# First expert's rows of the last batch summed into PSUM, and scatters moved to one unit of a group

## The chip, the cores and the metric

The kernel runs on one core of a Trainium2 chip. The metric is the device time of one execution in microseconds (us). The five engines are PE (TensorE: matmuls and weight loads), DVE (VectorE), ACT (ScalarE), POOL (GpSimd) and SP (SyncE, which here only issues DMAs). TensorE runs at one of two clock levels, 1.2 or 2.4 GHz; the profile's PEclk is the granted share of 2.4 GHz.

## The reference, cut to what matters

```
x = x + attention(layernorm(x))      # x: 4 batches x 512 tokens x 256, 32 query heads, 8 KV heads
y = layernorm(x)                     # mixture of experts, 8 experts, top 2
gates = softmax(y @ gating_w); topk_w, topk_idx = top_k(gates, 2)
position = running count of the items of an expert, in token order; valid = position < 640
buf[expert, position] = y[token]     # 8 experts x 640 slots x 256
h = relu(buf @ w1 + b1); out_e = h @ w2 + b2
out = x + sum over the token's two experts of weight * out_e[expert, position]
```

An expert has CAP = 640 slots. A slot holds a token's normalised row (256 numbers), its token number and the gate weights of the 8 experts (ROW = 265 numbers). The slots of the first expert, number 0, are rows 0 to 639 of the DRAM tensor slot_rows.

## The kernel before

**Attention.** The work goes in 32 groups (4 batches x 8 KV heads, g = 0 to 31) of 16 units each; a unit is 128 query rows of one head. The function all_periods (line 331) writes the order out by hand: in unit n of group g every engine runs its step for n of this group, for n - 16 of the next group, for n + 16 of the group before and for n + 32 of the one before that. So projections of the next group (PE, lines 1298 to 1329), the rotations of its query and key chunks (POOL, lines 614 to 630), and the product of probabilities and values of the group before (PE, line 1383, in units 4, 6 and 8) lie among the scores of this group (PE line 1365, DVE lines 1021 and 1030, ACT line 765). Rotation Q23 lies in unit 2, KV and Q01 of the next group in units 4 and 5. POOL's residual addition (line 659) of an earlier group lies in unit 6, the sink term (line 642) in unit 15, the denominator (line 652) in unit 0 after it. On ACT the sink's exponential (line 785) stands in unit 15.

**Routing.** While batch b + 1 is in attention, the steps route(r, b) with r = 0 to 121 run beside it, r = 16 * (g % 8) + unit: transposes (line 1452), statistics, gate logits (line 1464), top 2, the count of items per expert (PE lines 1475 to 1481), the slot numbers (DVE lines 1172 to 1196), the gate weights (line 1197) and the normalised rows (ACT line 895). Then POOL scatters the rows into slot_rows with eight indirect DMAs of 128 rows (line 676). SCATTER_AT places them, two at a time: r = 99 and 115 are unit 3 of the seventh and eighth group, r = 105 and 121 their unit 9. For the last batch nothing is left to run beside, so line 347 runs r = 0 to 121 one after the other with last = True.

**Experts.** After the last scatter has landed, SP loads the 640 rows of expert 0 (line 541), then those of expert 1, and the weights of expert 1 (lines 550, 553). PE runs two matmuls that only keep its clock up (line 1493), transposes the rows into banks 0 to 2 (turn_slots, line 1502), ACT and DVE split them into a high and a low part (slots_hi line 940, slots_lo line 1249), and PE makes the hidden layer (to_hidden, line 1524), transposes the rows of the next expert, and makes the output rows (to_rows, line 1537). DVE adds b2 (line 1268), ACT multiplies by the gate weight (line 958) and POOL adds the rows to the output with indirect DMAs (line 709). The slots of expert e + 1 are loaded once the rows of expert e - 1 have been added (line 540). On DVE, hidden_split (lines 1258, 1260) stands beside to_hidden.

## Time and profile before

| | us |
|---|---|
| median of 3 runs (1098.31 to 1101.82) | 1098.95 |
| the profiled execution's own time | 1099.66 |
| its span, first to last instruction | 1097.9 |
| PE busy, share of the span | 1041.9, 95% |
| DVE busy | 869.7, 79% |
| POOL busy | 706.1, 64% |
| ACT busy | 654.5, 60% |

The spans are counted from the first instruction. Attention ends at about 813 us, the routing of the last batch lies between about 817 and 837 us, and the experts fill the rest. A busy share is a mean over these three parts, so it says little of any of them; what matters is which wait ends last in each.

### The profile page before, as it was taken

How to read it: one execution, taken by the hardware profiler on the slowest of the kernel's cores; microseconds unless marked ns; L12 is line 12 of the kernel's file. 1: busy time of each engine (PE TensorE's matmuls, PEld its weight loads, DVE VectorE, ACT ScalarE, POOL GpSimd, SP SyncE). 2: the span in 40 equal slices, each digit the busy share in tenths (PEclk: the TensorE clock that was granted, in tenths of full speed). 3: DMA queues.
4: the chain of work that ended last, by engine and by line, in shares of the span. 5: the costliest groups of instructions: out<-in, count | busy, mean ns of one | idle time of the engine just before them, and what ended most of it. 6: DMA issues, size and time to landing. Idle time of an engine off the chain costs nothing.

```text
span 1097.9 us, 32754 instructions
## 1 busy us (share of the span) xinstructions
PE 1041.9 (95%) x13282; PEld 747.8 (68%) x13282; DVE 869.7 (79%) x1929; ACT 654.5 (60%) x1662; POOL 706.1 (64%) x586
## 2 busy tenths in 40 slices
PE   7999999999999999999999999999883999999995
PEld 4466666666666666666666666666562999999995
DVE  7999999999899999999998999898861455555441
ACT  4666667666677666676766666676631555545441
POOL 5658766767666787666788676667732454555662
PEclk9999999999999999999999999999996999999998
DMA  4555554433333333432334333232524044444321
GB/s 111 155 132 127 132 145 123 125 90 96 93 84 95 102 98 80 118 79 77 85 104 119 85 99 97 68 91 73 161 77 156 18 118 122 121 122 112 90 59 21
DMA packets 115399, 111.46 MB, mean 102 GB/s; under 512 B 35216, under 2 KB 103888, under 8 KB 115120
## 3 DMA queue, kind: packets, MB, share of 16 engines
q1 hardware_dynamic: 97504, 89.61, 29.8%
q0 software_dynamic: 7296, 8.55, 4.7%
q10 hardware_dynamic: 10448, 11.20, 3.5%
q8 instruction: 105, 1.72, 0.7%
q14 instruction: 46, 0.38, 0.1%
HBM read 74.17 MB, written 21.83 MB: 87 GB/s over the span
## 4 chain that ended last, share of the span: by engine, by line
PE 53%; DVE 37%; issue 4%; DMA 2%; ACT 1%; POOL 1%; SPq 0%; POOLq 0%; DVEq 0%
PE bank L1383 20%; DVE probs_ring L1021 16%; DVE probs_t L1030 14%; PE bank L1365 10%; PE bank L1537 9%; PE bank L1524 9%; DVE heads_sb L1050 4%; PE bank L1502 1%; PE bank L1415 1%; PE bank L1307 1%; DMA slots<-slot_rows 1%; PE bank L1324 1%; PE bank L1342 1%; POOL out L709 1%; PE bank L1464 1%
## 5 line engine op out<-in xcount | busy, mean ns | idle before, releaser
L765 ACT ACTIVATE probs_ring<-probs_ring,neg_max 128x512 f32<-128x512 f32 x512 | 365.8, 717 | 227.0 <-DVE neg_max L1021 220.1
L1021 DVE CUSTOM_DVE_ANT_0 probs_ring<-bank,mask,sink_neg 128x512 f32<-128x512 f32 x512 | 360.0, 736 | 31.9 <-PE bank L1365 30.3
L1030 DVE STREAM_TRANSPOSE probs_t<-probs_ring 128x1024 f32<-128x1024 f32 x256 | 317.2, 1239 | 0.2 <-ACT probs_ring L765 0.2
L1365 PE MATMUL bank<-qk_st 64*128 64x512 f32 x1024 | 281.2, 625 | 12.7 <-DVE neg_max L1021 8.1
L1383 PE MATMUL bank<-probs_t,v_quads 32*64 32x256 f32 x8192 | 254.5, 381 | 1.5 <-DVE probs_t L1030 0.7
L1383 PEld LDWEIGHTS bank<-probs_t,v_quads 32*64 32x64 f32 x8192 | 181.9, 132 | 81.9 <-issue 54.5
L624 POOL TENSOR_TENSOR chunk_sb<-chunk_sb,rope_sb 128x512 f32<-128x512 f32 (+1 forms) x94 | 119.8, 1274 | 128.3 <-issue 100.4
L1365 PEld LDWEIGHTS bank<-qk_st 64*128 64x128 f32 x1024 | 85.2, 186 | 78.3 <-DVE neg_max L1021 43.1
L629 POOL TENSOR_TENSOR qk_st<-chunk_sb,swap_sb 128x512 f32<-128x512 f32 (+1 forms) x94 | 120.2, 1279 | 7.4
L1415 PEld LDWEIGHTS bank<-wo_sb,heads_sb 64*128 64x128 f32 x992 | 96.1, 187 | 37.5 <-issue 29.2
L625 POOL TENSOR_TENSOR swap_sb<-swap_sb,rope_sb 128x512 f32<-128x512 f32 (+1 forms) x94 | 120.0, 1276 | 0.0
L1415 PE MATMUL bank<-wo_sb,heads_sb 64*128 64x256 f32 x992 | 117.4, 376 | 0.0
L1537 PE MATMUL bank<-w_part,hidden_hi 128*128 128x256 f32 x640 | 115.6, 284 | 0.0
L1324 PE MATMUL bank<-xcur,w_hi 64*128 64x512 f32 x496 | 100.6, 479 | 0.0
L682 POOL TENSOR_TENSOR w_lo<-w_raw,w_hi 128x2048 fp32r<-128x2048 f32 x8 | 36.9, 4609 | 96.6 <-ACT w_hi L844 96.6
L1537 PEld LDWEIGHTS bank<-w_part,hidden_hi 128*128 128x128 f32 x640 | 98.7, 189 | 0.1
L765 ACT ACTIVATION_READ_ACCUMULATOR probs_ring<-probs_ring,neg_max 128x1 f32 x512 | 97.2, 190 | 0.0
L950 ACT ACTIVATE hidden<-bank,b_sb 128x320 f32<-128x320 f32 x128 | 60.5, 524 | 54.1 <-PE bank L1524 54.1
L1537 PE MATMUL bank<-w_part,hidden_lo 128*128 128x256 f32 x320 | 90.5, 283 | 0.0
L1268 DVE TENSOR_TENSOR expert_sb<-bank,b_sb 128x256 f32<-128x256 f32 x40 | 17.0, 424 | 82.7 <-PE bank L1537 75.4
L659 POOL TENSOR_TENSOR x_sb<-x_sb,y_sb 128x512 f32<-128x512 f32 x62 | 79.2, 1277 | 4.5
L709 POOL DMA_INDIRECT out<-expert_sb,slots x40 | 64.1, 1602 | 26.9 <-ACT expert_sb L958 17.2
(162 smaller groups left out, 1474.5 us busy)
## 6 DMA issues: line engine op xcount, KB each, us to landing
v_quads<-v_rows SPq DMA_DIRECT2D x128, 128.0 KB
recip_wide<-recip_rows SPq DMA_DIRECT2D x64, 256.0 KB
w_raw<-in_L_ffn_w SPq DMA_DIRECT2D x14, 1024.0 KB, 8.4
swap_sb<-chunk_sb SPq DMA_DIRECT2D x314, 32.0 KB
w_raw<-in_L_attn_W_qkv SPq DMA_DIRECT2D x32, 256.0 KB, 2.9
slot_rows<-x2T ACTq DMA_DIRECT2D x8, 662.5 KB, 5.8
slots<-slot_rows SPq DMA_DIRECT2D x8, 662.5 KB, 4.0
w_raw<-in_L_attn_W_qkv SPq DMA_DIRECT2D x64, 64.0 KB, 2.8
```

Of the source, the lines that this page charges most:

```text
L624: nc.gpsimd.tensor_tensor(straight, straight, rope_sb[rows, 0, :], ALU.mult).then_inc(s_pool, 1)
L625: nc.gpsimd.tensor_tensor(swapped, swapped, rope_sb[rows, 1, :], ALU.mult).then_inc(s_pool, 1)
L629: nc.gpsimd.tensor_tensor(qk_st[j][rows, PAIRS if c == KV else c - Q01, :], straight, swapped, ALU.add).then_inc(s_rot, 1)
L765: nc.scalar.activation(probs[(g * UNITS + n) % RING][:, :], probs[(g * UNITS + n) % RING][:, :], ACT.Exp, bias=neg_max[j][:, n:n + 1], sca ...
L1021: nc.vector.tensor_tensor_reduce(probs[(g * UNITS + n) % RING][:, :], SCORE[SCORE_OF[n // 2][n % 2]][:, :], mask[:, L - P - t * P:2 * L - ...
L1030: nc.vector.transpose(probs_t[j][:, :, (h // 2) * (2 * P):(h // 2 + 1) * (2 * P)] .rearrange("p b (h q) -> p h b q", h=2)[:, :, :, t * BLK ...
L1324: ins = nc.tensor.matmul(chunk_bank(c)[:, :], w[rows, kc, chunk_cols(c)], xcur[g // NKV % 2][rows, part, kc, :], start=(second == 0 and kc ...
L1365: nc.tensor.matmul(SCORE[SCORE_OF[n // 2][hh]][:, :], qk_st[j][half, h // 2, t * P:(t + 1) * P], qk_st[j][half, PAIRS, :], start=True, sto ...
L1383: ins = nc.tensor.matmul(PV[a][p * HD:(p + 1) * HD, 0:2 * P], v_quads[j][rows, d, c * HD:(c + 1) * HD], probs_t[j][rows, blk, p * 2 * P:(p ...
L1415: ins = nc.tensor.matmul(PV[a][:, 0:D], heads_sb[rows, a, h * P:(h + 1) * P], wo_sb[rows, (g % NKV) * 2 + h, :], start=(half == 0 and h == ...
L1524: ins = nc.tensor.matmul(banks[4 + 2 * (c % 2) + half][:, 0:HALF], w[:, kc, c * P:(c + 1) * P], a[:, at:at + HALF], start=(kc == 0 and m = ...
L1537: ins = nc.tensor.matmul(FFN2[s][:, 0:D], a[:, c, s * P:(s + 1) * P], w[:, c, :], start=(c == 0 and m == 0), stop=(c == HC - 1 and m == 2))
```

## The change

In words. (1) After the scatters of the first three batches have landed, SP loads the rows of expert 0 that are in slot_rows by then (slots[0], "old rows"). In the last batch's routing PE fills banks 0 to 2 with zeros by a product with a zero column and adds the transposes of the old rows, written as ordinary fp32 products with the identity. (2) DVE makes a 0/1 matrix for each of the four tiles of the last batch (select, 128 tokens x 640 slots: 1 where the token's slot in expert 0 equals the slot number, which POOL writes with an iota). ACT makes the high part of the normalised rows (last_hi) and DVE the low part (last_lo). PE multiplies both by select and adds them into the same banks: 8 times 4 matmuls. So banks 0 to 2 hold what turn_slots(0) gave before, and to_hidden(0) no longer waits for the scatters, the load or the transposes of expert 0. (3) The rows of expert 1 are loaded first once the last scatter has landed, and expert 0's full rows (for token numbers and gate weights) behind them. (4) The weights of expert 1 are loaded before the scatters are waited for. b1 is loaded and transposed earlier, b1 and b2 have semaphores of their own. (5) The two keep_warm matmuls ahead of turn_slots(0) are gone. (6) SCATTER_AT puts two scatters in r = 89 and three each in r = 105 and 121, all of them unit 9 of a group (the sixth, seventh and eighth). (7) In SBUF slots and qk_st[0] are placed elsewhere.

```diff
-        SCATTER_AT = {99: (0, 1), 105: (2, 3), 115: (4, 5), 121: (6, 7)}
+        SELECT_AT = 72
+        SCATTER_AT = {89: (0, 1), 105: (2, 3, 4), 121: (5, 6, 7)}
...
             recip_out(GROUPS - 2)
             recip_spread(GROUPS - 2)
+            sp.wait_ge(s_rot, GROUPS * CHUNKS)
+            sp.dma_start(b1_rows[:, :], b1.rearrange("e (c p) -> (e c) p", p=P)).then_inc(s_b1_in, 16)
+            sp.wait_ge(s_scores, (GROUPS - 1) * UNITS)
+            sp.wait_ge(s_scattered, (B - 1) * (16 * TPB * TOPK))
+            sp.dma_start(slots[0][:, :, :], slot_rows_of(0)).then_inc(s_old_in, 16)
             recip_out(GROUPS - 1)
             recip_spread(GROUPS - 1)
             out_init(B - 1)
...
+            weights_in(1)
 
             sp.wait_ge(s_scattered, 16 * TILES * TOPK)
+            slots_in(1)
+            sp.wait_ge(s_slots_turned, 3)
             slots_in(0)
-            sp.wait_ge(s_slots_in[0], 16)
-            for e in range(E - 1):
-                slots_in(e + 1)
...
+            for e in range(2, E):
+                slots_in(e)
+                weights_in(e)
...
             def pool_route(r, b, last):
+                if r == TURN_X_LAST and last:
+                    pool.wait_ge(s_residual, 2 * GROUPS)
+                    nc.gpsimd.iota(slot_numbers[:, :].rearrange("p (s q) -> p s q", s=SLOTT), pattern=[[1, SLOTT], [SLOTT, P]],
...
                 if r == WEIGHTS_AT and last:
-                    norm2(b, 0)
+                    for t in range(TPB):
+                        norm2(b, t)
+                        nc.scalar.activation(last_hi[:, t, :], x_sb[:, b * TPB + t, :], ACT.Identity,
+                                             bias=norm_bias[:, t:t + 1], scale=rstd[:, t:t + 1]).then_inc(s_last_hi, 1)
                     act.wait_ge(s_neg_top, b + 1)
                     nc.scalar.activation(gates[:, :, :], gates[:, :, :], ACT.Exp).then_inc(s_gate_exp, 1)
-                    for t in range(1, TPB):
-                        norm2(b, t)
...
             def weigh(e):
+                if e == 0:
+                    act.wait_ge(s_slots_in[0], 16)
...
+                if r == SELECT_AT and last:
+                    dve.wait_ge(s_place, b + 1)
+                    step(nc.vector.scalar_tensor_tensor(place_key[:, :], prefix[:, :, 0], 1.0,
+                                                        chosen[:, :, 0].bitcast(F32), ALU.add, ALU.mult))
+                    dve.wait_ge(s_slot_numbers, 1)
+                    for t in range(TPB + 1):
+                        if t < TPB:
+                            nc.vector.tensor_scalar(select[:, t, :], slot_numbers[:, :], place_key[:, t:t + 1], None,
+                                                    ALU.is_equal).then_inc(s_select, 1)
+                        if t > 0:
+                            dve.wait_ge(s_norm2, b * TPB + t)
+                            dve.wait_ge(s_last_hi, t)
+                            nc.vector.tensor_tensor(last_lo[:, t - 1, :], xn2[:, t - 1, 0:D],
+                                                    last_hi[:, t - 1, :].bitcast(F32), ALU.subtract).then_inc(s_last_lo, 1)
...
+            def old_rows(bank):
+                nc.tensor.matmul(banks[bank][:, :], ones_r[:, :], before_r[:, 0:1].broadcast_to([P, 512]),
+                                 start=True, stop=False)
+                for m in range(bank * 4, min(bank * 4 + 4, KC * SLOTT)):
+                    kc, s = divmod(m, SLOTT)
+                    nc.tensor.matmul(slot_cols(kc, s, s + 1), slots[0][:, s, kc * P:(kc + 1) * P], identity[:, :],
+                                     start=False, stop=False)
+
+            SLOT_PIECES = [(0, 0, 4), (0, 4, 5), (1, 0, 3), (1, 3, 5)]
+
+            def last_rows(t, part):
+                rows = (last_hi, last_lo)[part]
+                for i, (kc, s0, s1) in enumerate(SLOT_PIECES):
+                    final = t == TPB - 1 and part == 1
+                    ins = nc.tensor.matmul(slot_cols(kc, s0, s1), rows[:, t, kc * P:(kc + 1) * P],
+                                           select[:, t, s0 * P:s1 * P], start=False, stop=final and i != 1)
...
             def pe_route(r, b, last):
+                if r == LOGITS_AT + 1 and last:
+                    pe.wait_ge(s_old_in, 16)
+                    pe.wait_ge(s_residual, 2 * GROUPS)
+                    old_rows(0)
+                    old_rows(1)
+                if r == SELECT_AT and last:
+                    pe.wait_ge(s_centred, B)
+                    old_rows(2)
+                    for i in range(2 * TPB):
+                        t, part = ((0, 0), (1, 0), (0, 1), (2, 0), (1, 1), (3, 0), (2, 1), (3, 1))[i]
...
-            pe.wait_ge(s_bias_in, 32)
-            pe.wait_ge(s_place, B)
-            nc.tensor.transpose(PV[3][:, 0:E * HC], b1_rows[:, :], identity[0:E * HC, 0:E * HC]).then_inc(s_b1_turned, 1)
-
-            pe.wait_ge(s_scattered, 16 * TILES * TOPK)
-            keep_warm(2, PROJ, x_sb[:, 0:2, :])
-
...
-            turn_slots(0)
             pe.wait_ge(s_b1, 1)
```

## Rows read from the trace of the kernel before

**Rows 1.** The page, chain that ended last, shares by engine.
```profile
PE 53%; DVE 37%; issue 4%; DMA 2%; ACT 1%; POOL 1%; SPq 0%; POOLq 0%; DVEq 0%
```

**Rows 2.** Chain of waits from last routing to first output rows: start, us, what.
```profile
824.25 0.19 DVE prefix L1175
...
826.41 0.20 DVE xn L370
...
839.13 3.97 DMA slots<-slot_rows
...
846.83 14.33 PE bank L1524 x96
...
861.30 1.28 PE bank L1502 x10
862.58 14.24 PE bank L1537 x120
```

**Rows 3.** Timeline of POOL: a scatter in group 31; first and last of the last batch.
```profile
785.70 1.00 POOL L676 DMA_INDIRECT slot_rows<-xn,scatter_idx  x1
...
827.55 1.00 POOL L676 DMA_INDIRECT slot_rows<-xn,scatter_idx  x1 [20.21 <-DVE xn L370]
...
836.57 0.98 POOL L676 DMA_INDIRECT slot_rows<-xn,scatter_idx  x1 [0.30 <-issue]
```

**Rows 4.** Timeline of PE: last output projection, and logits of the last routing.
```profile
813.53 3.72 PE L1404 MATMUL bank<-wo_sb,heads_sb 128*128 128x256 f32 x16 [0.92 <-DVE heads_sb L1050]
...
818.59 1.91 PE L1464 MATMUL bank<-gate_sb,x2T 128*128 128x8 f32 x16
```

**Rows 5.** Busy time by window; the eighth value (PEclk) is TensorE's granted clock.
```profile
821.00:822.00 1.00, 0.00 (x0) 0.00 (x0) 0.93 (x11) 0.98 (x2) 0.00 (x0) 0.50 0.77 270
...
844.00:845.00 1.00, 1.00 (x8) 1.00 (x6) 0.01 (x1) 0.60 (x1) 0.00 (x0) 0.58 0.89 164
```

**Rows 6.** Lines 1258 and 1260 on DVE: duration in ns, min/median/max.
```profile
L1258 DVE CAST hidden_hi<-hidden x64: 493/494/682, 849.8 to 1072.6; 128x640 fp32r<-128x640 f32 x64
...
L1260 DVE TENSOR_TENSOR hidden_lo<-hidden,hidden_hi x64: 824/826/849, 850.4 to 1073.1; 128x640 fp32r<-128x640 f32 x64
```

**Rows 7.** Timeline of ACT: normalised rows of the last batch.
```profile
823.85 0.60 ACT L895 ACTIVATE xn<-x_sb,norm_bias,rstd 128x256 f32<-128x256 f32 x1 [1.32 <-DVE norm_bias L1160]
...
824.51 1.57 ACT L895 ACTIVATE xn<-x_sb,norm_bias,rstd 128x256 f32<-128x256 f32 x3
```

**Rows 8.** Line 709 on POOL, the scatter-adds beside the experts, ns min/median/max.
```profile
L709 POOL DMA_INDIRECT out<-expert_sb,slots x40: 1544/1554/1907, 874.7 to 1087.8; - x40
```

**Rows 9.** Timeline of POOL, the sink term once in a group: start of groups' ends.
```profile
358.31 0.21 POOL L642 TENSOR_TENSOR sink_arg<-neg_max,sink_all 128x16 f32<-128x16 f32 x1 [2.94 <-DVE neg_max L1021]
...
407.98 0.21 POOL L642 TENSOR_TENSOR sink_arg<-neg_max,sink_all 128x16 f32<-128x16 f32 x1 [0.91 <-DVE neg_max L1021]
...
431.87 0.21 POOL L642 TENSOR_TENSOR sink_arg<-neg_max,sink_all 128x16 f32<-128x16 f32 x1 [2.12 <-DVE neg_max L1021]
...
554.62 0.21 POOL L642 TENSOR_TENSOR sink_arg<-neg_max,sink_all 128x16 f32<-128x16 f32 x1 [1.61 <-DVE neg_max L1021]
...
604.39 0.21 POOL L642 TENSOR_TENSOR sink_arg<-neg_max,sink_all 128x16 f32<-128x16 f32 x1 [0.82 <-DVE neg_max L1021]
...
752.46 0.22 POOL L642 TENSOR_TENSOR sink_arg<-neg_max,sink_all 128x16 f32<-128x16 f32 x1 [1.63 <-DVE neg_max L1021]
...
803.05 0.21 POOL L642 TENSOR_TENSOR sink_arg<-neg_max,sink_all 128x16 f32<-128x16 f32 x1 [0.84 <-DVE neg_max L1021]
```

**Rows 10.** Timeline of PE: probability-value products, without and with scatters just before.
```profile
417.50 2.41 PE L1383 MATMUL bank<-probs_t,v_quads 32*64 32x256 f32 x80
...
786.82 3.51 PE L1383 MATMUL bank<-probs_t,v_quads 32*64 32x256 f32 x80
```

**Rows 11.** Timeline of ACT behind the sink term of group 16, without scatters.
```profile
432.85 0.20 ACT L785 ACTIVATE sink_exp<-sink_arg 128x16 f32<-128x16 f32 x1
...
436.56 0.60 ACT L747 ACTIVATE chunk_sb<-bank 128x512 f32<-128x512 f32 x1 [1.30 <-PE bank L1324]
```

More of the change, by code:

```diff
@@ L246, in moe_layer @@
         v_next = sb("v_next", [P, TPB, HD], c=actx)
-        qk_st = [sb(f"qk_st{i}", [P, PAIRS + 1, L], c=actx) for i in range(2)]
+        qk_st.append(sb("qk_st1", [P, PAIRS + 1, L], c=actx))
         v_quads = [sb(f"v_quads{i}", [P, TPB, TPB * HD], c=actx) for i in range(2)]
@@ L274, in moe_layer @@
         b1_sb = sb("b1_sb", [P, E, HC], c=mctx)
+        sb("behind_rope", [P, 320], c=mctx)
+        slots = [sb(f"slots{i}", [P, SLOTT, ROW], c=mctx) for i in range(2)]
         b2_sb = sb("b2_sb", [P, E, D], c=mctx)
@@ L277, in moe_layer @@
         w2_hi, w2_lo = w2_parts[0::2], w2_parts[1::2]
-        slots = [sb(f"slots{i}", [P, SLOTT, ROW], c=mctx) for i in range(2)]
         slots_hi = sb("slots_hi", [P, KC * CAP], F32R, c=mctx)
@@ L281, in moe_layer @@
         hidden = [sb(f"hidden{i}", [P, CAP], c=mctx) for i in range(2)]
+        lctx = ExitStack()
+        slot_numbers = sb("slot_numbers", [P, CAP], c=lctx)
+        place_key = sb("place_key", [P, TPB], c=lctx)
+        select = sb("select", [P, TPB, CAP], F32R, c=lctx)
+        last_hi = sb("last_hi", [P, TPB, D], F32R, c=lctx)
+        last_lo = sb("last_lo", [P, TPB, D], F32R, c=lctx)
+        lctx.close()
         hidden_hi = sb("hidden_hi", [P, HC, CAP], F32R, c=mctx)
@@ L1265, in rows_out @@
                     dve.wait_ge(s_added, e * SLOTT * 16)
+                else:
+                    dve.wait_ge(s_b2_in, 16)
                 for s in range(SLOTT):
@@ L1437, in _, with slot_cols @@
             turn_v(0)
-            def pe_route(r, b, last):
+            def slot_cols(kc, s0, s1):
+                m = kc * SLOTT + s0
+                return banks[m // 4][:, m % 4 * P:(m % 4 + s1 - s0) * P]
+            def old_rows(bank):
[12 more added lines that the diff above has]
+                                           select[:, t, s0 * P:s1 * P], start=False, stop=final and i != 1)
+                    if final and i != 1:
+                        ins.then_inc(s_slots_turned, 1)
+            def pe_route(r, b, last):
+                if r == LOGITS_AT + 1 and last:
[8 more added lines that the diff above has]
+                        t, part = ((0, 0), (1, 0), (0, 1), (2, 0), (1, 1), (3, 0), (2, 1), (3, 1))[i]
+                        if part == 0:
+                            pe.wait_ge(s_select, t + 1)
+                            pe.wait_ge(s_last_hi, t + 1)
+                        else:
+                            pe.wait_ge(s_last_lo, t + 1)
+                        last_rows(t, part)
                 if r in TURN_X_AT:
```

51 lines of the change are left out of this document (33 added, 18 removed).

## The prediction

> **What bounds the kernel now.** I read the page first: its chain of waits lies on PE and DVE for 90% of the span and on DMA, POOL and issuing for a few per cent [rows 1]. These few per cent are what the change is about, so I went to the chain in order of time. Behind the last attention group it runs over DVE's routing to the slot numbers (824.25) and the gate weights, which end at 826.61, then over eight scatters on POOL, their landing, the load of expert 0's rows (839.13 to 843.10), their transposes, and reaches the first hidden matmul at 846.83; the output rows of expert 0 start at 862.58 [rows 2]. The eight scatters are issued 1.288 us apart, from 827.55 to 836.57 [rows 3], and the load starts at 839.13, so from gate weights to landed scatters it is 12.5 us, and 4.0 more for the load. PE does nothing useful in it.
>
> The second place is in attention. A group takes 23.89 us from one sink term to the next where nothing is scattered (407.98 to 431.87, group 16). Groups 14 and 15 take 49.67 together, 22 and 23 take 49.77, 30 and 31 take 50.59 [rows 9]. Twice 23.89 is 47.78, so the three pairs of groups in which scatters stand cost 1.89, 1.99 and 2.81 us extra, 6.69 in all. Where it is lost is seen on PE: a block of 80 probability-value matmuls takes 2.41 us in group 16 and 3.51 in group 31 [rows 10], where the first scatter of unit 3 had been issued at 785.70, 1.1 us before the block [rows 3]. PE waits for no semaphore inside such a block; the rows show when the stall comes, not what makes it. That is 1.1 us a hit, and a hit in each of the six groups gives 6.6 of the 6.69.
>
> **Part one, the last batch.** I count on the clock of the profiled execution, with attention unshifted.
>
> Old rows on PE begin at 820.50, when the logits end [rows 4]. The nearest row is line 1404: eight fp32 matmuls (16 records) of 256 columns in 3.72 us [rows 4], 0.465 each. A 128-column one is taken as half, 0.23; eight are 1.9 us. Two fills of 512 columns cost 0.24 each, from 14.24 us for 120 matmuls of 256 columns [rows 2]. Sum 2.3 us, to 822.8, just when the count can start anyhow. But the granted clock fell to 0.50, the 1.2 GHz level, by 821 [rows 5], after PE had done nothing but transposes and 8-column matmuls since 817. At that level the old rows take up to 4.7 us and count and slot numbers come up to 1.9 us later. At the lower end, nothing. I take 0.7, nearer to the low end because the new matmuls fill the very stretch in which PE stood still before.
>
> Then DVE, on which all the new work stands ahead of picks, indices and gate weights. Slot numbers end at 824.44 [rows 2], plus 0.7 is 825.15. place_key is a small instruction, 0.2. Four select instructions go by the 128x640 cast, 0.52 with issue; upper bound is the 128x640 two-operand form, 0.83 [rows 6], which would add 1.2 us. Four last_lo of 128x256 go by the same two-operand row, 0.83 cut from 640 to 256 columns by the sum of a fixed part and a column part: about 0.38. Sum 3.6, to 828.95. ACT must not be later: norm rows and last_hi are eight activations at 0.52, from 823.85 [rows 7], so the last last_hi is ready at 828.05; the exponential of the gates behind them ends at 828.3, before DVE asks for it. POOL's iota waits for the last residual at 818 and has six us of cover; its price if late is its own length, about 1 us. So DVE ends last_lo at 828.95 instead of beginning the picks at 824.47: all that followed there, 2.14 us to the gate weights, now ends at 831.1, 4.5 us later than 826.61.
>
> PE meanwhile: eight last_rows of 1280 columns, at 0.119 per 256 columns 0.6 each; the last two need the last lo part, so PE ends at about 830.2. ACT's three hi parts follow; DVE's three lo parts come behind the gate weights, 831.1 plus 1.7 (1280 columns, twice the 128x640 form [rows 6]), so the hidden layer can begin at 832.8 instead of 846.83. It takes 14.33 [rows 2], to 847.1.
>
> The scatters are still there and start 4.5 us later: the load that started at 839.13 starts at 843.6, and its rows, now expert 1's, are in at 847.6. **Both paths meet within half a us**, and the later one counts: transposes of expert 1 (1.28 [rows 2]) from 847.6, output rows of expert 0 at 848.9 instead of 862.58. That is **13.7 us** gained. It is not the 14 us of the transfer that vanish: the transfer is there, but it lies beside expert 0's hidden layer. What comes behind has the same order and the same spacing as before, so the 235 us from there on stay. Expert 0's full rows are loaded right behind expert 1's and are wanted first when its rows are weighed, over 14 us later.
>
> Costed at nothing: the weights of expert 1, 2 MB. By the load of 662 KB in 3.97 us [rows 2] they need about 12.6 us; issued near 820 they are in at 833, beside the first scatters, and are first read after expert 0's hidden layer at 847. If they held up the scatters, each us is a us of the end. b1's transpose lies in front of the last probability-value block, where PE waits for DVE. The load of the old rows stands on SP ahead of the last reciprocals' DMA; it waits for the third batch's scatters, issued by 792, and the reciprocals are due at 805. If those scatters landed after 805, the heads would be late by the difference. The two keep-warm matmuls lay beside the load, so nothing is gained by leaving them out; what they did, the new matmuls must do. Before, the clock was granted at 0.50 until it came back between 844 and 845 [rows 5], ahead of the first hidden matmul.
>
> **Part two, the scatters.** Those of unit 3 go; nothing replaces them there. Unit 9 now has two in groups 13, 21, 29 and three in the six groups from 14 on. A scatter costs POOL 1.29 [rows 3], three are 3.9 us. In group 16 POOL stood idle for 2.12 us before its sink term [rows 9], so it is 1.8 late with three. ACT reads the sink term 0.77 after its end (432.08 to 432.85), and 3.7 us later ACT waits 1.30 us for PE [rows 11]: of 1.8 late, 0.77 is slack and the remaining 1.0 falls into those 1.30. So I charge nothing; the bound above is 1.0 in five groups, 5.0 us. In group 31 POOL has no rotations left and reaches unit 9 early, when PE is still in its last block; I leave one hit there, 1.1. So part two gives 6.69 - 1.1 = **5.6 us**; the lower bound is 0.6, with the lateness above charged in full.
>
> **Sum.** 13.7 + 5.6 = 19.3 us. On the profiled execution's own 1099.66 (span 1097.9 and 1.8 around it) that is 1080.4; the median of the runs stands 0.7 lower, so 1079.7.
>
> **Two rules weighed.** The stalls of rows 10 stand in a block of many short instructions. The Trainium skill (Runtime: NRT & Kernel Launch, Instruction fetch mechanics) says of instruction fetch that it is hidden because the sequencer dispatches more slowly than its buffer fills. By that rule moving a DMA could not speed PE by way of the fetch; the rows show a us lost there whatever its name, and by the rule alone part two would give nothing.
>
> The new scatters run beside DVE's hidden split, the old ones beside an idle DVE. The nearest row is line 709: 40 indirect DMAs in the expert part, median 1554 ns, longest 1907 [rows 8]; at the longest, eight scatters lose 8 x 0.35 = 2.8 us, my upper bound. The Trainium skill (SBUF — State Buffer, The "DVE blocks DMA" trap, with its figures under A bandwidth-pool intuition that's wrong) says that such a DMA cannot get its descriptors written while DVE runs a copy of the two-port kind, and gives about 3.1 us instead of 0.62. An estimate by that page is 8 x 3.1 in place of 8 x 1.29, 14.5 us more, with 1094 as the end. Rows 8 speak against it.
>
> **Rivals.** (a) Part one as told, part two gives nothing or the third scatter's lateness comes through: 1079.7 + 5.0 to 5.6, about **1085**. For it: POOL's idle time is smaller than three scatters. Against: two scatters of unit 9 already left only 0.9 idle and cost no more [rows 9]. (b) The clock stays at 1.2 GHz through the last rows: 8 x 0.6 becomes 8 x 1.2 and starts near 827, hidden layer at about 838.5, its first us also slow, a loss of 6 to 7: **1086**. For it: the clock fell at just this place [rows 5]. Against: PE is now busy almost without a break. (c) **Slower.** POOL's scatters are held by DVE's hidden split beside them, in the 14 us of expert 0's hidden layer. Expert 1's rows then come late and PE waits ahead of turn_slots(1). It decides from 19.3 / 8 = 2.4 us more per scatter; at 4.0 us each, 8 x 2.7 = 21.7 lost: **1101**. (d) It does not do what it says: the old rows or the b1 wait hold PE past the scatters' landing, so that part one gives nothing: 1099.66 - 5.6 - 0.7 = **1093**; the loads would have to be 10 us late.
>
> **Chances.** Forecast 0.73, (a) 0.14, (b) 0.07, (c) 0.03, (d) 0.03. The range 1076.0 to 1086.0 takes in (a) and (b); below, it has part one without the 0.7, both paths at their best (0.6), part two in full (1.1) and a stall or two less in the expert part. About 0.3% (3.3 us) can be told from no change. Faster 0.96, same 0.01, slower 0.03.
>
> **What would show it.** First hidden matmul near 833 minus part two's shift of 5.6, so 827; the output rows of expert 0 near 843; transposes of expert 1 waiting for their load by less than 1 us; scatters of the last batch 1.3 us apart. Blocks of 80 in groups 14, 15, 22, 23 back at 2.4 to 2.7 us, groups at 23.9. Wrong would be: sink terms that ACT waits for, the granted clock at 0.50 beyond 826, scatters over 1.6 us apart, or a long wait for expert 1's slots.

## The result: 1086.97 us, 1.2% faster, and 7 us short of the forecast

| | kernel before | changed kernel |
|---|---|---|
| median of the runs on the same chip | 1100.24 us (1098.31 to 1101.82, 4 runs) | 1086.97 us (1085.54 to 1088.03, 4 runs) |
| span of the profiled execution | 1097.9 us | 1086.2 us |
| mean granted TensorE clock | 0.981 | 0.988 |

Ratio 0.9879, 95% interval 0.9856 to 0.9903. The direction was right; the time lies 0.97 us above the range.

The span is 11.7 us shorter. It can be cut in three, at the start of the last heads_sb products (the end of attention) and at expert 0's first output product. The stretch in between went from 49.62 to 37.62 us (12.0 less, 13.7 forecast), attention became 1.4 us **longer** (812.72 to 814.15, 5.6 less forecast), and what follows 1.2 us shorter (235.58 to 234.42, nothing forecast). So part one nearly came, and attention as a whole shows nothing of part two.

The shares of the chain on the changed kernel's page, beside [rows 1] ("issue" is time in which an engine waited for nothing that the profile shows):

```profile
PE 58%; DVE 32%; issue 4%; POOL 2%; SPq 1%; ACT 1%; DMA 1%; POOLq 0%; another core or an unknown queue 0%; DVEq 0%
```

The changed kernel's chain of waits from the old rows to expert 0's output rows (start, us, what), beside [rows 2]:

```profile
824.60 1.30 PE bank L1507 x8
...
826.27 0.20 DVE prefix L1214
...
826.70 0.56 DVE select L1228
...
827.31 5.38 PE bank L1516 x32
832.69 2.04 issue
834.74 15.87 PE bank L1615 x96
850.60 0.14 issue
850.74 1.29 PE bank L1593 x10
852.02 1.06 PE bank L1628 x9
```

The 3.97 us load has left the chain, as said. But the hidden layer (L1615) takes 15.87 us instead of 14.33. TensorE's clock by window (the eighth value), beside [rows 5]:

```profile
822.00:823.00 1.00, 1.00 (x5) 0.91 (x5) 0.83 (x8) 0.86 (x3) 0.00 (x0) 0.50 1.17 245
...
825.00:826.00 1.00, 1.00 (x11) 1.00 (x9) 0.67 (x5) 0.72 (x2) 0.00 (x0) 0.84 0.94 361
...
836.00:837.00 1.00, 1.00 (x5) 1.00 (x5) 0.00 (x0) 0.00 (x0) 0.69 (x2) 0.50 0.19 68
838.00:839.00 1.00, 1.00 (x6) 1.00 (x5) 0.41 (x1) 0.56 (x2) 0.86 (x1) 0.51 0.37 136
839.00:840.00 1.00, 1.00 (x8) 1.00 (x8) 0.92 (x2) 0.00 (x0) 0.69 (x2) 1.00 0.26 98
```

It was full again by 826, then fell to 1.2 GHz once more at 836 to 839, behind the 2.04 us in which PE stood idle ahead of the layer. The scatters, now beside DVE's hidden split (timeline of POOL, beside [rows 3]; the last line is the view of line 745, beside [rows 8]):

```profile
832.98 1.00 POOL L712 DMA_INDIRECT slot_rows<-xn,scatter_idx  x1 [12.71 <-DVE xn L390]
834.29 0.98 POOL L712 DMA_INDIRECT slot_rows<-xn,scatter_idx  x1 [0.30 <-issue]
...
841.11 1.28 POOL L712 DMA_INDIRECT slot_rows<-xn,scatter_idx  x1 [0.30 <-issue]
842.70 0.98 POOL L712 DMA_INDIRECT slot_rows<-xn,scatter_idx  x1 [0.31 <-issue]
...
L745 POOL DMA_INDIRECT out<-expert_sb,slots x40: 1543/1558/1903, 864.1 to 1076.1; - x40
```

The seven steps from one scatter to the next are 1.28 to 1.60 us: 0.7 us lost in all, nowhere near rival (c).

Group 31, where attention lost its time. ACT and ACT's queue at the sink term, and PE's value blocks, beside [rows 10, 11]:

```profile
778.00 0.22 ACT L821 ACTIVATE sink_exp<-sink_arg 128x16 f32<-128x16 f32 x1 [2.17 <-issue]
778.01 0.37 ACTq L901 DMA_DIRECT2D w_raw<-in_L_ffn_w  x1
```

```profile
779.79 1.13 PE L1420 MATMUL bank<-qk_st 64*128 64x512 f32 x4 [2.07 <-DVE neg_max L1060]
780.85 4.10 PE L1441 MATMUL bank<-probs_t,v_quads 32*64 32x256 f32 x80
...
785.94 3.26 PE L1441 MATMUL bank<-probs_t,v_quads 32*64 32x256 f32 x55
789.97 1.14 PE L1441 MATMUL bank<-probs_t,v_quads 32*64 32x256 f32 x25 [0.77 <-issue]
...
792.94 3.62 PE L1441 MATMUL bank<-probs_t,v_quads 32*64 32x256 f32 x96
```

The third scatter of group 30 makes its sink term late, ACT waits 2.17 us for it, and ACT's 1 MB load of the second weights goes out 2.2 us into group 31 (0.7 ahead of it before). The first three blocks of value products of group 31 take 4.10 us, 5.17 (the two pieces with their gap) and 3.62; undisturbed they take 2.41, 2.41 and 2.85. My first reading joined these two facts; the experiments parted them.

### The profile page after: what moved, and what is told of

It is laid out like the page before. It is cut to its first block, busy times and chain, and to the rows that moved or that the text cites. A ratio compares the mean times of both kernels' runs of the same rounds, so it can differ in the third digit from the quotient of the medians.

```text
span 1086.2 us, 32862 instructions
## 1 busy us (share of the span) xinstructions
PE 1042.8 (96%) x13323; PEld 753.0 (69%) x13323; DVE 874.8 (81%) x1938; ACT 657.7 (61%) x1666; POOL 708.7 (65%) x587
## 3 DMA queue, kind: packets, MB, share of 16 engines
q0 software_dynamic: 7296, 8.55, 4.8%
q8 instruction: 105, 1.72, 0.7%
## 4 chain that ended last, share of the span: by engine, by line
PE 58%; DVE 32%; issue 4%; POOL 2%; SPq 1%; ACT 1%; DMA 1%; POOLq 0%; another core or an unknown queue 0%; DVEq 0%
PE bank L1441 18%; DVE probs_ring L1060 14%; DVE probs_t L1069 12%; PE bank L1615 11%; PE bank L1628 10%; PE bank L1420 10%; DVE heads_sb L1089 3%; PE bank L1473 2%; PE bank L1379 1%; PE bank L1362 1%; PE bank L1593 1%; PE bank L1562 1%; PE bank L1397 1%; SPq L474 1%; ACT probs_ring L801 1%
## 5 line engine op out<-in xcount | busy, mean ns | idle before, releaser
L1060 DVE CUSTOM_DVE_ANT_0 probs_ring<-bank,mask,sink_neg 128x512 f32<-128x512 f32 x512 | 360.1, 736 | 31.9 <-PE bank L1420 28.9
L1441 PE MATMUL bank<-probs_t,v_quads 32*64 32x256 f32 x8192 | 249.4, 382 | 1.4 <-issue 0.8
```

The costliest lines, as they stand in the source:

```text
L1060: nc.vector.tensor_tensor_reduce(probs[(g * UNITS + n) % RING][:, :], SCORE[SCORE_OF[n // 2][n % 2]][:, :], mask[:, L - P - t * P:2 * L - ...
L1441: ins = nc.tensor.matmul(PV[a][p * HD:(p + 1) * HD, 0:2 * P], v_quads[j][rows, d, c * HD:(c + 1) * HD], probs_t[j][rows, blk, p * 2 * P:(p ...
```

## The experiments

Ratios are to the kernel before on the same chip; "near 1100" and "near 1093" are the medians that this kernel had there. Groups are measured from the first DVE instruction of one to that of the next, group 31 to the last heads_sb. "Five groups" are 14, 15, 22, 23 and 30. "Clock" is the time that a stretch lost to a granted clock under 1 (the sum of one minus the clock over its windows; one stay of 3.41 us at 0.50 counts 1.71). "Hidden to rows" runs from expert 0's first hidden product to its first output product.

| kernel | chip | ratio [95%] | five groups | group 31 | clock in 31 | attention to rows | hidden to rows |
|---|---|---|---|---|---|---|---|
| before | 1100 | | 124.65 | 34.03 | 0 | 49.62 | 15.51 |
| r0_before | 1100 | | 124.69 | 37.68 | 1.71 | 49.15 | 15.50 |
| e7_no_packets | 1100 | 0.9991 [0.9971, 1.0011] | 124.61 | 35.27 | 1.71 | 50.45 | 17.00 |
| r2_before | 1093 | | 119.42 | 35.42 | 3.42 | 49.74 | 15.52 |
| e2_places_alone | 1093 | 1.0011 [0.9985, 1.0036] | 119.59 | 35.02 | 3.42 | 50.37 | 16.86 |
| e2b_places_alone | 1093 | 1.0005 [0.9986, 1.0024] | 119.01 | 31.94 | 0 | 49.23 | 15.51 |
| changed | 1100 | 0.9879 [0.9856, 0.9903] | 122.46 | 38.38 | 3.41 | 37.62 | 17.04 |
| r1_after | 1093 | 0.9881 [0.9861, 0.9902] | 118.72 | 33.71 | 1.71 | 37.61 | 17.04 |
| r2_after | 1093 | 0.9876 [0.9856, 0.9897] | 118.74 | 32.01 | 0 | 37.63 | 17.05 |
| r3_after | 1093 | 0.9877 [0.9849, 0.9906] | 118.73 | 33.56 | 1.71 | 37.60 | 17.04 |
| e1_old_places | 1093 | 0.9884 [0.9862, 0.9906] | 119.27 | 35.23 | 0 | 37.17 | 17.07 |
| e1b_old_places | 1093 | 0.9900 [0.9877, 0.9923] | 119.17 | 33.59 | 1.71 | 37.13 | 17.04 |
| e1c_old_places | 1100 | 0.9898 [0.9855, 0.9941] | 125.01 | 34.47 | 0 | 37.95 | 17.85 |
| e3_third_behind_sink | 1093 | 0.9872 [0.9843, 0.9902] | 119.60 | 31.94 | 0 | 37.62 | 17.04 |
| e3b_third_behind_sink | 1100 | 0.9895 [0.9850, 0.9939] | 120.71 | 37.02 | 3.41 | 38.17 | 18.07 |
| e4_w2_load_earlier | 1100 | 0.9886 [0.9850, 0.9922] | 122.40 | 38.38 | 3.41 | 41.21 | 20.62 |
| e5_keep_warm | 1100 | 0.9886 [0.9857, 0.9914] | 120.96 | 37.34 | 3.42 | 37.98 | 17.86 |
| e6_third_and_warm | 1100 | 0.9885 [0.9847, 0.9923] | 123.38 | 35.94 | 1.71 | 37.94 | 17.84 |
| e8_warm_last_group | 1100 | 0.9858 [0.9822, 0.9894] | 121.20 | 34.35 | 0 | 37.93 | 17.82 |
| e8b_warm_last_group | 1093 | 0.9866 [0.9836, 0.9895] | 118.76 | 32.18 | 0 | 37.21 | 17.11 |

**The two parts apart.** The changed kernel as it is, with the old places (e1), and the kernel before with the new places (e2):

```diff
-        SCATTER_AT = {89: (0, 1), 105: (2, 3, 4), 121: (5, 6, 7)}
+        SCATTER_AT = {99: (0, 1), 105: (2, 3), 115: (4, 5), 121: (6, 7)}
```

> The changed kernel once more, beside the three that follow. Theory T: the last batch's part gains 12 us, and the moved scatters give back what they win, so 12 to 14 us below the kernel before. In its trace the blocks of 80 value products stand at 2.4 to 2.7 us in groups 14, 15, 22, 23, 30, and group 31 is again over 36 us long (34.0 before) because the load of w2 is issued 2 us into it. Rival R: the long group 31 was chance; then it is 32 to 34 us here and the gain is 4 us larger.

> The changed kernel with the scatters in their old places, units 3 and 9, two at a time. T: the moved scatters are worth nothing in sum, since 4 us are lost in group 31; so this runs within 1.5 us of the changed kernel, its groups 14, 15, 22, 23, 30 each about 1 us longer and group 31 about 4 us shorter. Prediction's part two, if only its size was missed (P): this is 3 to 6 us slower than the changed kernel.

> The kernel before with the scatters in their new places and nothing else. T: 0 to 2 us from the kernel before in either direction, group 31 some 4 us longer than before and the earlier groups with scatters shorter. P: 5.6 us faster, 1094.

On this chip, near 1093, part one alone is the gain (1080.94 us of the chip's 1092.54, where the whole change has 1080.54); the places alone give nothing. In r1_after group 31 took 33.71 us instead of over 36, and the ratio was the same: neither that group's length nor a gain of 4 us came as the two readings wanted. And with the old places the five groups took 119.3 us, not 124.7: the pauses that part two was to remove were not in this profile. Was that the chip or the new last batch?

**The third scatter behind the sink term** (in the third batch's last place, unit 9 of group 31, all three stay together; the third scatter of group 30 moves):

```diff
-        SCATTER_AT = {89: (0, 1), 105: (2, 3, 4), 121: (5, 6, 7)}
+        SCATTER_AT = {89: (0, 1), 105: (2, 3), 111: (4,), 121: (5, 6), 127: (7,)}
+        SCATTER_THIRD = {89: (0, 1), 105: (2, 3), 111: (4,), 121: (5, 6, 7)}
-        ROUTE_STEPS = 122
+        ROUTE_STEPS = 128
-                for c in SCATTER_AT.get(r, ()):
+                for c in (SCATTER_THIRD if b == B - 2 else SCATTER_AT).get(r, ()):
```

> The changed kernel with each third scatter moved from unit 9 to unit 15, where POOL stands between the sink term and the denominator (for the third batch only in its first group of three). T: POOL is on time for the sink term, ACT issues the load of w2 before group 31 starts, group 31 falls back to 33 to 34 us, and groups 14, 15, 22, 23 to 23.9 us or less; 4 to 7 us faster than the changed kernel, about 1081. Rival R: the lateness of POOL was not the cause; within 1 us of the changed kernel.

It was 2.8 us below r1_after on the same chip, where 4 to 7 were expected, with group 31 at 31.94. The repeat undid that:

> The changed kernel with the third scatter of each place put behind the sink term. On the first chip it was 2.8 us shorter than the changed kernel, and its group 31 had no fall of the clock (31.9 us). If that came from the sink term's time, it is again 0.985 to 0.987 and ScalarE's load of the second weights is issued within 0.3 us of group 31's start; if from the luck of the clock in one profile, 0.988, with the load as early and group 31 at 33.6 to 38.4.

ACT's load was as early (0.42 us ahead of group 31), group 31 took 37.02 and the ratio was 0.9895. The first gain can't be told from chance: 0.9872 and 0.9881 each lie in the other's interval.

**The pauses: chip, places or packets.** The kernel before again; and with a bound of 0 on the slot numbers of the first three batches, so that these tokens' rows are not written (that part of the computation is left out). The name e7_no_packets says too much: the queue moved 7296 packets in it as in r0_before, but 2.19 MB instead of 8.55, since 256 of a batch's 384 packets shrank from 4240 bytes to 16:

```diff
-                        xn2[:, c // TOPK, :], None, bounds_check=E * CAP - 1, oob_is_err=False).then_inc(s_scattered, 16)
+                        xn2[:, c // TOPK, :], None, bounds_check=E * CAP - 1 if last else 0, oob_is_err=False).then_inc(s_scattered, 16)
```

> The kernel before, unchanged, profiled once more. If the pauses of TensorE at the third heads of groups 14, 15, 22, 23 and 30 (24.80 to 25.22 us a group in its first profile, where the kernel with the new last batch but the old places took 23.53 to 24.01) come from the places of the scatters, they are there again: these five groups sum to about 124.7 us. If they belong to the one execution that the prediction was read from, the five sum to 119.0 to 120.0 us, the span is the shorter by nearly as much, and the 6.7 us that the prediction wanted back were never lost as a rule. Group 27: 27.6 us in either case, as in both kernels with the last batch of before; 25.9 would say that its 1.7 us are chance too.

> The kernel before, with a bound of 0 for the slot numbers of every batch's scatters but the last one's: POOL issues them as before and makes their descriptors, but the tokens' rows of these batches are not written (those slots keep other data; the products on them take the same time). If the pauses of a group with scatters come from their packets beside the loads, groups 14, 15, 22, 23 and 30 take 23.5 to 24.0 us, group 31 31 to 33 us. If they come from POOL's time, they are as in the other runs of this kernel on this chip, and the time is within 1 us of the kernel before.

> The kernel before, profiled a third time, on the chip of the three runs beside it. In its two profiles so far, and in that of the run without the packets, groups 14, 15, 22, 23 and 30 summed to 124.7, 124.7 and 124.6 us. On the chip where all four kernels with old or new places took 118.7 to 119.6 for them, no profile of this kernel was taken. If the pauses are a matter of the kernel and its places, the five sum to 124.7 here whatever the chip; if of the chip, this sum goes with the chip's time: near 124.7 where the kernel's median is near 1100, 119 to 120 where it is near 1092. Group 31 took 34.0 and 37.7 us in the two profiles: here anything from 34 to 38.

The second block of group 14, in the kernel before on a chip near 1100 (r0_before, timeline of PE):

```profile
363.25 2.41 PE L1383 MATMUL bank<-probs_t,v_quads 32*64 32x256 f32 x80
367.02 3.63 PE L1383 MATMUL bank<-probs_t,v_quads 32*64 32x256 f32 x80
```

the same block on a chip near 1093 (r2_before), the same source:

```profile
364.87 2.41 PE L1383 MATMUL bank<-probs_t,v_quads 32*64 32x256 f32 x80
368.64 2.49 PE L1383 MATMUL bank<-probs_t,v_quads 32*64 32x256 f32 x80
```

So the length of the pause goes with the chip: five groups 124.7 us in both profiles of this kernel near 1100, 119.4 near 1093. Without the rows' bytes it stays (124.61), so the bytes do not make it; the small packets and POOL's work on the descriptors were still there, and are not tested. It does go with the places, on such a chip:

> The new last batch with the old places. On a chip whose kernel before is near 1100: if the places are worth what the five groups show, these sum to 124.7 us and the ratio is 0.990 to 0.991, 2 to 3.5 us above the changed kernel's 0.988; if not, 0.988. On a chip near 1093: 0.988 to 0.990 as in the two runs there, five groups at 119.3 to 119.6.

```profile
368.77 3.42 PE L1441 MATMUL bank<-probs_t,v_quads 32*64 32x256 f32 x80
```

That is group 14 of e1c; the changed kernel has 2.41 there. Old places give 124.6 to 125.0 in four profiles near 1100, new ones 120.7 to 123.4 in six (e3b and e6 among them, with the third scatter behind the sink term): 1.2 to 4.3 us, not 5.6. This block sorts old and new places on every chip: with the old ones it took 3.32 to 3.63 us near 1100 and 2.49 to 2.57 near 1093, with the new ones 2.41 in all 13 profiles.

In the changed kernel's profile no value block of the five groups is longer than undisturbed, yet groups 15 and 23 took 25.31 and 25.03 us. They lose it at the turn to the next group. PE's records end the scores at 408.60, and DVE gets them 1.3 us later:

```profile
407.58 1.02 PE L1420 MATMUL bank<-qk_st 64*128 64x512 f32 x4
409.96 0.75 DVE L1060 CUSTOM_DVE_ANT_0 probs_ring<-bank,mask,sink_neg 128x512 f32<-128x512 f32 x1 [1.27 <-PE bank L1420]
```

Near 1093 (r2_after) DVE has no such wait there. And such a chip has pauses where nothing is scattered: group 3 took 25.30 us in the changed kernel, 25.67 in e4 and 24.84 in e8, and 23.86 to 23.90 in all ten profiles near 1093. What makes these pauses, what a scatter adds to them, and why one chip shows them and another does not, stays open. The same four kernels on one chip near 1093:

> The changed kernel once more. Ratio to the kernel before 0.988 as on two chips (13.3 and 12.0 us less); the five groups 121 to 122.5 us where the kernel before has 124.7, or 118.7 where it has under 120; group 31 33.7 to 38.4; last batch, from the end of attention to expert 0's output rows, 37.6 us where the kernel before has 49.6.

> The changed last batch with the places of the scatters as before. If the places are worth nothing anywhere, within 1 us of the changed kernel, as on the first chip that ran both. If the places are worth the 2 to 4 us that the five groups show on the chip of 1100 us, it is 1 to 4 us slower there than the changed kernel, with the five groups at 124.7. If they are worth less than nothing, because the third scatter makes ScalarE's load of the second weights late, it is 1 to 3 us faster, with group 31 at 34 to 36 against 37 to 38.

> The kernel before with the new places alone. The prediction's part two said 5.6 us faster than the kernel before. If the five groups give 2 to 4 us and group 31 takes none of it back: ratio 0.997, 3 us faster. If group 31 takes it back: ratio 1.000 within 0.002. If on a chip where the pauses aren't there: 1.001 as the first time.

The places alone again gave nothing (1.0005). Beside the new batch the old ones came out 3.9 us slower in the median, with intervals that overlap; the two profiles, 5.6 us apart, show 1.7 in group 27 and 1.6 in group 31, both falls of the clock, and 0.4 in the five groups. Over all chips the four runs of the change have 0.9876 to 0.9881 and the three with old places 0.9884 to 0.9900: all told the places are worth some 0 to 2 us. On a chip near 1100, where most was to be won, the old and the new places were never run beside each other with all else equal, so what they are worth there comes from the profiles and from ratios of different chips.

**Group 31: the load, or the clock.** The load of the second weights one unit earlier:

```diff
-        W1_IN_AT, W2_IN_AT = LAST - 3, LAST - 1
+        W1_IN_AT, W2_IN_AT = LAST - 3, LAST - 2
```

> The changed kernel with ScalarE's 1 MB load of expert 0's second weights issued one unit earlier, some 3 us, all else as it was. Theory: group 31 is long because this load comes up against the value blocks of its first heads, and the more so the later it is issued (at -0.74 us from the group's start the group took 34.0, at -0.04 31.9, at 0.8 to 1.4 33.7 to 35.2, at +2.23 38.4). Then group 31 takes 31 to 34 us and the kernel 0 to 3 us less than the changed one (ratio to the kernel before 0.985 to 0.988). Rival: group 31 is long by what the last batch's own scatters and loads need, and the time of the load decides nothing: 33.7 to 35.2 us as before, within 1 us of the changed kernel. Second rival: earlier, the load meets group 30's value blocks and the pause only moves: group 30 up from 23.5 to 25 to 27 us, the sum of the two as before.

The load went out 1.96 us ahead of the group and group 31 took 38.38 us, to the hundredth what the changed kernel took with the load at +2.23. The theory of the load fell. The granted clock and the chip sort the profiles instead. Windows of the changed kernel in group 31:

```profile
780.00:781.00 1.00, 1.00 (x12) 0.24 (x18) 0.94 (x3) 1.00 (x4) 1.00 (x2) 0.97 0.67 196
781.00:782.00 1.00, 1.00 (x24) 0.77 (x29) 1.00 (x2) 1.00 (x4) 0.92 (x2) 0.50 0.99 342
782.00:783.00 1.00, 1.00 (x26) 0.66 (x20) 1.00 (x5) 1.00 (x4) 1.00 (x2) 0.50 1.08 370
783.00:784.00 1.00, 1.00 (x32) 0.77 (x24) 1.00 (x3) 1.00 (x2) 1.00 (x1) 0.50 0.41 112
784.00:785.00 1.00, 1.00 (x34) 0.50 (x20) 0.18 (x1) 1.00 (x4) 0.86 (x2) 0.82 0.00 0
```

A stay at 0.50 counts 1.71 us; it comes once, twice or not at all. Where it does not come and PE does not pause in a block either, the group takes 31.9 to 32.0 us (e2b, e3, r2_after). With 1.71 us taken off for each stay, nine of the ten profiles near 1093 have 31.6 to 32.2 us (e1, with a pause in its blocks, 35.23), and the ten near 1100 have 33.6 to 36.0, old and new places alike. So the pauses of this group, too, go with the chip, and the new places do not take them away. At the head of the group PE stands idle twice between the scores of the first heads, in every profile without added products: 0.8 to 1.3 us and 1.7 to 2.5 us. It does so in the six where no fall came as well, so the idle time alone does not decide it. One product of no use behind each of these scores:

```diff
+                    if g == GROUPS - 1 and n in (0, 2):
+                        pe.wait_ge(s_chunk_out, GROUPS * CHUNKS)
+                        keep_warm(1, PROJ, x_sb[:, 0:2, :])
```

> The changed kernel with one product of no use on TensorE behind the scores of the first and of the second head of group 31, in the 0.84 and 1.72 us that it stands idle there for DVE. Theory (the idle time lets the clock fall): no stretch at 0.50 in group 31, the group at 31.9 to 32.1 us in the profile (on a chip with the pauses up to 34), where without the products four profiles of five of kernels with the new last batch showed 33.6 to 38.4 in it with a fall or a stall and two 31.9 to 32.0; the median 1 to 3 us below the changed kernel's 0.988, so a ratio of 0.985 to 0.987, and the spread of its runs smaller. Rival: the falls come whatever is put there: group 31 at 33.6 to 38.4 with a stretch at 0.50 in it, ratio 0.988. Second rival: the products delay the second head's scores by their own time, and what the clock gives they take: 0.987 to 0.989.

> The changed kernel with the two products of no use at the head of group 31, a second time, beside the changed kernel itself. Theory: again no stretch at 0.50 in group 31; the group at 31.9 to 32.1 us on a chip near 1093, 34 to 34.5 on one near 1100; the median 1.5 to 4 us under that of the changed kernel beside it. Rival (the first time was luck): a stretch at 0.50 in group 31, or none in either, and medians within 1 us.

> The changed kernel beside it, ratio 0.988 to the kernel before as on three chips (0.9879, 0.9881, 0.9876). Group 31 with one or two stretches at 0.50 in it and 33.7 to 38.4 us (two profiles of three so far), or with none and 32.0 (one of three).

PE at the head of group 31 in e8:

```profile
774.41 1.12 PE L1404 MATMUL bank<-x_sb,identity 128*128 128x512 f32 x2
775.47 1.13 PE L1420 MATMUL bank<-qk_st 64*128 64x512 f32 x4
776.52 1.12 PE L1404 MATMUL bank<-x_sb,identity 128*128 128x512 f32 x2
778.18 1.13 PE L1420 MATMUL bank<-qk_st 64*128 64x512 f32 x4 [0.53 <-DVE neg_max L1060]
779.24 2.41 PE L1444 MATMUL bank<-probs_t,v_quads 32*64 32x256 f32 x80
```

and its windows there:

```profile
779.00:780.00 1.00, 1.00 (x34) 0.65 (x39) 1.00 (x2) 1.00 (x2) 1.00 (x1) 1.00 0.95 248
...
781.00:782.00 1.00, 1.00 (x27) 0.48 (x13) 1.00 (x3) 1.00 (x2) 1.00 (x2) 1.00 0.36 116
```

The second score pair now waits for nothing, the third 0.53 us. No stay at 0.50 in group 31 in either profile; 12 of the 18 profiles without the products have one. That alone could be chance: at a third without, two in a row happen one time in nine. The medians go the same way: 1078.07 against 1079.47 us for r3_after on the same chip (1.4 less, just short of the 1.5 to 4 expected), and the lowest two ratios of the study. The intervals overlap, so this version is likely, not shown, to beat the change.

**The first hidden layer.** Two such products between the last prefix row and that layer:

```diff
             all_periods(pe, pe_step, pe_route, pe_ahead)
+            pe.wait_ge(s_b1, 1)
+            keep_warm(2, PROJ, x_sb[:, 0:2, :])
```

> The changed kernel with a few products of no use put on TensorE between the last product of the prefix rows and the first hidden layer, where it stood idle for 2.0 us and its granted clock fell to 0.50 for 3 us of the hidden layer (15.87 us where the kernel before took 14.33). Theory: the idle time let the clock fall; filled, the hidden layer takes 14.3 to 14.6 us and the rows of expert 0 begin 1.3 to 1.5 us sooner, the kernel 0.5 to 1.5 us shorter (ratio 0.985 to 0.988). Rival: the clock falls whatever is put there, for the low clock follows from the time before (822 to 825 us): the hidden layer stays at 15.6 to 15.9 us, and the time within 0.3 us. Second rival: the added products are still running when the slots' numbers are there, and what the clock gives they take: hidden layer short but begun 1 us later.

> The changed kernel with the third scatter behind the sink term and the products of no use ahead of the first hidden layer. Theory: the first hidden layer takes 14.3 to 14.4 us to its last product (15.5 us to expert 0's rows, where all undisturbed profiles without the products show 17.04), and the kernel is 1.5 us shorter than the same kernel without these products, run beside it. Rival: ScalarE pauses twice for 1 to 2 us in that layer, as it did with these products the first time, and nothing is gained: 17 to 18 us, ratios equal.

The clock stayed at 1.00 in both, but it had stayed so in that layer in four of the twelve profiles without these products too (e1, e1c, e8, e8b), so that the products held it is not shown. Nothing clear of noise was gained: e6 is 2.1 us under e3b in the median, with ratios of 0.9885 and 0.9895 and intervals that overlap, and from hidden layer to rows it took 17.84 us. That is the rival of e6. On two chips near 1100, ACT waited for products that PE's records show as done (e5, timeline of ACT):

```profile
842.81 0.95 ACT L987 ACTIVATE hidden<-bank,b_sb 128x320 f32<-128x320 f32 x2 [2.46 <-remote]
845.74 1.78 ACT L987 ACTIVATE hidden<-bank,b_sb 128x320 f32<-128x320 f32 x4 [1.98 <-remote]
```

DVE's part for these two steps was done in time (840.24 and 841.74), so it is PE's signal that was late. The same two waits stand in e6, e8 and e1c (the last two have no added products there): full clock, 16.64 to 16.68 us to the layer's end, 17.8 to 17.9 to the rows. (The 20.62 us of e4 hold two falls, 3.4 us, and 1.7 us more.) On chips near 1093 a layer at full clock took 14.31 us (e1, e8b), but then the other path decides. The chain of waits of e8b:

```profile
832.06 3.78 DMA slot_rows<-xn,scatter_idx
835.85 4.50 DMA slots<-slot_rows
840.35 0.04 issue
840.39 1.31 PE bank L1596 x10
841.71 1.32 PE bank L1631 x11
```

PE's last hidden product starts at 838.36 and PE waits 1.72 us for expert 1's slots. So hidden to rows takes 17.04 with a fall in this layer, where the layer ends last, and 17.07 to 17.11 in the two profiles near 1093 without one, where the load does. These two are also those in which the last scatter landed latest, 3.8 and 4.0 us after its issue, where the other profiles of the new last batch have 2.4 to 2.8. Whether that is chance is open, and with it whether a full clock would have gained up to 1.4 us elsewhere (the load was in at 35.05 in e1b). What bounds it then is the scatters and their load. Whether the load is quicker without expert 0's whole slots, sent 0.4 us behind it on the same queue, was not tried.

## Why the forecast missed: part two

**What was right.** In the last batch the load left the chain, both paths meet at expert 1's transposes (hidden to rows is 17.04 us where the layer decides and 17.07 to 17.11 where the load does), the scatters keep their pace beside DVE's split, and the loads of expert 1's weights and of the old rows are hidden. The sign asked of the blocks came too: all blocks of 80 in groups 14, 15, 22 and 23 took 2.41 us. Gate weights were said to end at 831.1; moved by attention's 1.4 us that is 832.5, and the first scatter started at 832.98. last_rows took 5.38 us where 8 x 0.6 was said.

**Part one, 13.7 said, 12.0 measured.** Counted from the end of attention, the hidden layer was said to begin at 20.08 us (832.8 less 812.72). It began at 20.59 in the changed kernel, whose clock had fallen on the old rows, and at 20.09 to 20.12 in the profiles where it had not (e1, e1b, e1c, e3b, e5, e6, e8, e8b): the path is right, the clock took 0.5. The layer then took 15.87 instead of 14.33, again the clock, 1.5. It ended 36.45 us after attention, while expert 1's rows were in at 35.24 where 34.9 was said. So in this profile the clock decided, and the load would have let PE begin about 1.2 us sooner (an estimate from these two numbers). In the two profiles whose layer nothing disturbed (e1, e8b) the load was in at 36.06 and 36.10 us, 1.2 later than said: in e8b it began at 31.6 where 30.9 was said and took 4.50 us where 4.0 was said. The shortest stretch from attention to rows in any profile is 37.13 us, 12.5 less than before. So two terms were mis-sized: the clock, taken at 0.7 in all and on the old rows alone, and the landing of the scatters with the load behind it. Of the 1.7 us missing, the load has between 0.3 and 1.2 and the clock the rest.

**Part two, 5.6 said, nothing to 2 measured: the step that failed.** It was "That is 1.1 us a hit, and a hit in each of the six groups gives 6.6 of the 6.69", taken from one profile and given, less one hit, to the change. Three things were wrong in it. First, the pauses are there at this length on a chip near 1100; near 1093 the five groups have 0.7 us of them in the kernel before. Second, where they are, moving the scatters clears the value blocks, but other pauses are left: groups 15 and 23 took 25.31 and 25.03 us, and of the five groups' 5.9 us over an undisturbed 118.7 the changed kernel's profile gives back 2.2. Third, the pauses of group 31 stay with the new places (2.0 us over an undisturbed 32.0 in the profile of the kernel before, 3.0 in the changed one's, falls taken off), where one hit of 1.1 had been left. Beside this, group 31 varies with the clock, by 1.71 us a fall, and that is luck of the profile: the kernel before happened to be profiled without a fall there (34.03; with one, 37.68), the changed one with two. Attention's +1.4 us is the sum of -2.2 (the five groups), +4.35 (group 31, 3.4 of it falls), -1.69 (group 27, where the profile of before had a fall), +1.83 (groups 2 and 3) and -0.9 (the rest). Rival (a), "part two gives nothing", was the one that came, at 2 us above its 1085.

**The third scatter's lateness, costed at nothing.** That held as far as can be told: at the end of group 15 ACT waits 0.69 us for the sink term in the changed kernel and 0.67 in r2_after, and the group took 25.31 us in the one and 23.91 in the other. In group 31 ACT did wait 2.17 us, and its load went 2.2 us late; e4, with the load early and group 31 as long, speaks against that costing anything, and so does r2_after, whose load went out 1.8 us late in a group of 32.01.

**The rule on fetching.** I named the Trainium skill (Runtime: NRT & Kernel Launch, Instruction fetch mechanics) for a rule by which part two would give nothing. Near 1093 it gave nothing, but since there was next to nothing to win; near 1100 moving the scatters did shorten the blocks, so the rule's conclusion for part two did not hold there. The fetch itself is a poor fit for these pauses: of the five in the profile of the kernel before, one (group 14) has a 16 KB packet of the instruction queue in flight for most of it, from 367.93 to 369.17, and those of groups 22, 23 and 30 have none. The rule of the Trainium skill that a DVE copy starves such DMAs (SBUF — State Buffer, The "DVE blocks DMA" trap) gives 3.1 us a scatter; 1.28 to 1.60 were measured.

**The tail.** 1.2 us less, nothing forecast: the kernel before waited 1.6 us for expert 4's slots (at 952), the changed one does not. All six profiles with the old last batch have this wait, 1.4 to 1.7 us, and none of the fourteen with the new one.

## What to carry to other kernels

A pause seen in one profile is worth its length only if it is there in a second profile, better on a second chip: profile the kernel before twice before a sum is built on it, and look at the granted clock of each stretch compared. Where the clock falls in some executions and not in others, two profiles differ by whole falls (1.5 to 1.7 us each here), which look like the effect of whatever was edited. When a transfer is moved beside work of equal length, work out both paths to the end: what the shorter one loses up to the difference is free, and what is saved on it is worth nothing.

## What the runs showed of the hardware

- A fall of the granted clock to 0.50 lasted 3.41 us or twice that in attention and the hidden layer. One of 3.41 us made group 27 1.7 us longer (25.93 to 25.94 or 27.62 us in every profile, nothing between) and the hidden layer 1.5 (14.3 to 15.9). In the same place it came in some executions and not in others.
- Chips differ: the same kernel has medians near 1093 on three chips and near 1100 on three. The profiles of the kernel before differ by 5.3 us of pauses of TensorE inside value blocks of 80 short products in five groups, and by 2 us or more of pauses in group 31. That such a pause is shorter with the scatters moved is shown; that it needs a scatter is not.
- On two chips near 1100, with a full clock and scatters beside the hidden layer, ACT waited for PE's signals of two of its eight parts 1.7 and 2.8 us beyond the end that PE's records give them; in group 15 of the changed kernel, near 1100 too, DVE waited 1.3 us in the same way. What held them is open.
